# Lag convolution as three half-length ones; patch transforms with 64 rows of weights for each dim

## The reference, cut to what matters

```
x = x + conv_of_rational_filter(gn(x))      # layer 0: full linear 2-D convolution, 16 x 16 channels
x = x + patch_layer(gn(x))                  # layer 1: 8x8 patches, queries, keys, values
x = x + conv3x3(gn(x))                      # layer 2
x = x + conv_of_rational_filter(gn(x))      # layer 3: as layer 0, other filters
```

```
X = rfft2(x, s=(256, 256)); Y = einsum('...hwi,ijhw->...hwj', X, h0 + rfft2(h)[0]); y = irfft2(Y)[:128, :128]
```

## Time and profile before

| | us |
|---|---|
| median of 3 runs | 4166.98 |
| profiled execution | 4160.19 |
| its span, first to last instruction | 4158.3 |
| granted TensorE clock, share of full speed | 0.952 |

### The profile page before, as it was taken

How to read it: one execution, slowest core, us unless ns; L and a number is a source line. 1 busy time by engine, 2 the same in 40 slices (tenths; PEclk the granted TensorE clock), 3 DMA queues, 4 the chain that set the end, 5 groups by cost and what they waited for, 6 DMA issues and landing times. The chain is left out here.

```text
span 4158.3 us, 76077 instructions
## 1 busy us (share of the span) xinstructions
PE 3687.6 (89%) x32456; PEld 2790.0 (67%) x32456; DVE 1537.0 (37%) x1765; ACT 1506.1 (36%) x1559; POOL 994.6 (24%) x1002
## 2 busy tenths in 40 slices
PE   8999999759999769999888979999889977798997
PEld 8888888726555557777577767777567764465655
DVE  7665656231111033333444453333454454211111
ACT  2665656521111024444343445445344431211110
POOL 6665656200000013333243003333234000000000
PEclk9999999979999879999999999999999998999998
DMA  2344444476554352212122432112121443855455
GB/s 68 115 133 128 135 128 136 133 211 182 141 163 140 98 149 80 81 40 81 41 81 66 131 109 81 60 61 81 41 63 65 111 128 42 214 154 162 140 143 131
DMA packets 223117, 462.62 MB, mean 111 GB/s; under 512 B 30042, under 2 KB 109156, under 8 KB 205036
## 3 DMA queue, kind: packets, MB, share of 16 engines
q1 hardware_dynamic: 211036, 437.18, 36.5%
q10 hardware_dynamic: 11792, 21.12, 1.6%
HBM read 341.32 MB, written 113.77 MB: 109 GB/s over the span
## 5 line engine op out<-in xcount | busy, mean ns | idle before, releaser
L648 PE MATMUL c_acc<-c_shifted,c_filt 128*32 128x512 f32 (+7 forms) x16384 | 957.4, 396 | 99.2 <-issue 62.8
L648 PEld LDWEIGHTS c_acc<-c_shifted,c_filt 128*32 128x32 f32 x16384 | 602.0, 137 | 456.1 <-issue 307.7
L700 ACT ACTIVATE c_filt<-c_filt 64x2048 f32<-64x2048 f32 (+1 forms) x64 | 121.9, 1905 | 826.2 <-DMA c_filt<-filters_dram 826.2
L240 PE MATMUL f_ab<-f_taps_ab,f_table 65*128 (+1 forms) x2080 | 296.4, 303 | 19.2 <-DMA f_table<-const_taps 8.2
L240 PEld LDWEIGHTS f_ab<-f_taps_ab,f_table 65*128 65x128 f32 x2080 | 277.8, 215 | 32.2 <-issue 22.7
L342 ACT ACTIVATE f_stage<-f_far 128x512 f32<-128x512 f32 x256 | 256.9, 1078 | 16.8 <-PE f_far L132 8.7
L664 DVE COPY c_filt<-c_filt 64x2048 f32<-64x2048 f32 (+1 forms) x64 | 77.6, 1213 | 480.2 <-DMA c_filt<-filters_dram 480.2
L125 POOL TENSOR_TENSOR q_w_q<-raw_weights,q_w_q 128x2048 fp32r<-128x2048 f32 x2 | 11.5, 5752 | 967.4 <-ACT q_w_q L121 967.4
L130 PE MATMUL q_acc_q<-xn,q_w_q 128*128 128x512 f32 x512 | 201.0, 393 | 40.0 <-DVE xn L125 40.0
L1104 POOL TENSOR_TENSOR sums<-sums,store 128x512 f32<-128x512 f32 x64 | 176.8, 2763 | 233.3 <-DVE store L1048 233.3
L405 DVE RECIPROCAL f_rec<-f_mag 128x256 f32<-128x256 f32 (+1 forms) x144 | 228.7, 1588 | 2.2 <-POOL f_mag L432 2.2
(11 more groups left out here) (181 smaller groups left out, 7772.3 us busy)
## 6 DMA issues: line engine op xcount, KB each, us to landing
c_shifted<-spectrum_dram SPq DMA_DIRECT2D x64, 1054.0 KB, 10.7
filters_dram<-f_stage SPq DMA_DIRECT2D x128, 512.0 KB, 4.1
c_filt<-filters_dram SPq DMA_DIRECT2D x64, 1024.0 KB, 8.2
raw_weights<-in_L_conv_Wk SPq DMA_DIRECT2D x16, 2048.0 KB, 8.2
raw_weights<-in_L_conv_Wv SPq DMA_DIRECT2D x16, 2048.0 KB, 8.2
o_raw<-in_L_conv_Wout SPq DMA_DIRECT2D x128, 256.0 KB, 3.7
f_table<-const_taps SPq DMA_DIRECT2D x120, 260.0 KB
raw_weights<-in_L_conv_Wq SPq DMA_DIRECT2D x15, 2048.0 KB, 8.2
```

The lines of the kernel that those rows point to most:

```text
L240: mm = nc.tensor.matmul(ab[blk % 2][:, k, part], table[:, blk % 2, k, part], taps_ab[:, q], start=True, stop=True)
L648: mm = nc.tensor.matmul(acc[k][32 * s:32 * s + 32, :, lag:L], filt[:, k, h, :, :, KB * s + kb].rearrange("p j c -> p (j c)"), shifted[:, k ...
```

## The change

```diff
 LAGS = 4
-ROW = L + LAGS
+HALF = L // 2
+ROW = 2 * (HALF + LAGS)
...
     ang = tau * np.outer(n, n) / L
-    inv_h = np.stack([np.cos(ang), np.sin(ang), -np.sin(ang)], 1)[:, :, ::-1] / L
+    lag_order = [8 * (15 - k) + 2 * (3 - l) + phase for k in range(16) for phase in range(2) for l in range(4)]
+    inv_h = np.stack([np.cos(ang), np.sin(ang), -np.sin(ang)], 1)[:, :, lag_order] / L
...
                 act.wait_ge(freq_ready, u + 1)
                 if u >= 4:
                     act.wait_ge(stored[u % 4], 32 * (u // 4))
-                nc.scalar.activation(rows[:, u % 4, :, LAGS:ROW], freq[u % 2][:], ACT.Copy).then_inc(rows_ready, 1)
+                nc.scalar.activation(rows[:, u % 4, :, :, LAGS:], freq[u % 2][:].rearrange("p b (t q) -> p b q t", q=2), ACT.Copy).then_inc(rows_ready, 1)
...
-def convolve(nc, layer, scratch, tag):
-
-
-    KB, RING, HALVES = L // 8, 4, 2
+def convolve(nc, layer, spare, scratch, tag):
+
+
+    KB, RING = HALF // LAGS, 4
+    N_BATCHES = GROUPS // RING
     RUN = 4 * B * ROW - LAGS
+    EVEN, ODD, SUM = range(3)
     with ExitStack() as ctx:
         sb, ps, sem = allocators(nc, ctx, tag)
-        filt = sb("filt", [128, RING, HALVES, C, 2, 4 * KB])
-        shifted = sb("shifted", [128, RING, 4, B, ROW])
-        out = sb("out", [128, RING, B, L])
-        acc = [ps(f"acc{k}", [128, B, L]) for k in range(RING)]
+        filt = sb("filt", [128, RING, 3, C, 2, 4 * KB])
+        shifted = sb("shifted", [128, RING, 4, B, 2, HALF + LAGS])
+        total = spare[:, 0].rearrange("p r n -> p (r n)").rearrange("p (k m t) -> p k m t", k=RING, t=HALF)
+        out = spare[:, 1].rearrange("p r n -> p (r n)")[:, 0:RING * B * L].rearrange("p (k b t q) -> p k b t q", k=RING, b=B, q=2)
+        odd = sb("odd", [128, 2, B, 1 + HALF])
+        both = sb("both", [128, 2, B, HALF])
+        acc = [[ps(f"acc{k}{phase}", [128, 2 * B, HALF]) for phase in range(3)] for k in range(2)]
         filt_in = [sem(f"filt_in{k}") for k in range(RING)]
         rows_in = [sem(f"rows_in{k}") for k in range(RING)]
-        group_done, acc_out = sem("group_done"), [sem(f"acc_out{k}") for k in range(RING)]
-        negated, copied, cleared = sem("negated"), sem("copied"), sem("cleared")
+        filt_summed, rows_summed, negated, copied, cleared = (sem(n) for n in (
+            "filt_summed", "rows_summed", "negated", "copied", "cleared"))
+        halves_done, group_done, odd_out, both_ready, acc_out = (sem(n) for n in (
+            "halves_done", "group_done", "odd_out", "both_ready", "acc_out"))
...
         def load(eng, g, k):
-            eng.dma_start(filt[0:64, k].rearrange("p h j c n -> p h (j c n)"),
-                          scratch["filters"][bass.ds(g, 1), :, 4 * layer:4 * layer + 4].rearrange("o (h p) q j n -> p (o h) (q j n)", h=HALVES)
+            eng.dma_start(filt[0:64, k, EVEN:SUM].rearrange("p h j c n -> p h (j c n)"),
...
-        def block_of(k, lower, column, first):
-
-            return filt[64 * lower:64 * lower + 64, k, :, :, column, KB * first:4 * KB].rearrange("p h j n -> p (h j) n")
+        def ahead(n, k):
+
+            return (n, 3) if k == 0 else (n + 1, k - 1)
+
+        def filters_of(k, phases, lower, column, first):
+
+            return filt[64 * lower:64 * lower + 64, k, phases, :, column, KB * first:4 * KB].rearrange("p h j n -> p (h j) n")
...
         @block.tensor
         def _(pe):
-            def groups(n):
+            def product(k, phase):
+                for kb in range(KB):
+                    for s in range(4):
+                        rows = total[:, k, B * s:B * s + B] if phase == SUM else shifted[:, k, s, :, phase]
+                        mm = nc.tensor.matmul(
+                            acc[k % 2][phase][32 * s:32 * s + 32, 0:B, LAGS * kb:HALF],
+                            filt[:, k, phase, :, :, KB * s + kb].rearrange("p j c -> p (j c)"),
+                            rows[:, :, 0:HALF - LAGS * kb], start=kb == 0, stop=kb == KB - 1)
+                return mm
+
+            def group(n, k):
+                pe.wait_ge(rows_in[k], 16 * (n + 1))
+                pe.wait_ge(negated, 2 * (RING * n + k) + 1)
+                pe.wait_ge(copied, 2 * (RING * n + k) + 1)
+                if isinstance(n, int) and n == 0:
+                    if k == 0:
+                        pe.wait_ge(cleared, 2)
+                    if k >= 2:
+                        pe.wait_ge(acc_out, k - 1)
+                else:
+                    pe.wait_ge(acc_out, RING * n + k - 1)
+                product(k, EVEN)
+                product(k, ODD).then_inc(halves_done, 1)
+                pe.wait_ge(negated, 2 * (RING * n + k) + 2)
+                pe.wait_ge(copied, 2 * (RING * n + k) + 2)
+                pe.wait_ge(rows_summed, RING * n + k + 1)
+                product(k, SUM).then_inc(group_done, 1)
+
+            for k in range(RING):
+                group(0, k)
+            with pe.Fori(1, N_BATCHES) as n:
...
-                    pe.wait_ge(rows_in[k], 16 * (n + 1))
-                    pe.wait_ge(negated, RING * n + k + 1)
-                    pe.wait_ge(copied, RING * n + k + 1)
-                    if isinstance(n, int):
-                        if k == 0:
-                            pe.wait_ge(cleared, 2)
-                    else:
-                        pe.wait_ge(acc_out[k], n)
-                    for kb in range(KB):
-                        for h in (1, 0):
-                            lag = 8 * kb + LAGS * (HALVES - 1 - h)
-                            for s in range(4):
-                                mm = nc.tensor.matmul(
-                                    acc[k][32 * s:32 * s + 32, :, lag:L],
-                                    filt[:, k, h, :, :, KB * s + kb].rearrange("p j c -> p (j c)"),
-                                    shifted[:, k, s, :, 0:L - lag], start=lag == 0, stop=lag == L - LAGS)
-                    mm.then_inc(group_done, 1)
-
-            groups(0)
-            with pe.Fori(1, GROUPS // RING) as n:
-                groups(n)
+                    group(n, k)
...
+        @block.gpsimd
+        def _(pool):
+            def sums(n, k):
+                pool.wait_ge(filt_in[k], 16 * (n + 1))
+                nc.gpsimd.tensor_tensor(filt[0:64, k, SUM], filt[0:64, k, EVEN], filt[0:64, k, ODD], ALU.add).then_inc(filt_summed, 1)
+                pool.wait_ge(rows_in[k], 16 * (n + 1))
+                rows = shifted[:, k].rearrange("p s b q t -> p (s b) q t")
+                nc.gpsimd.tensor_tensor(total[:, k], rows[:, :, 0, 0:HALF], rows[:, :, 1, 0:HALF], ALU.add).then_inc(rows_summed, 1)
+
+            for k in range(RING):
+                sums(0, k)
+            with pool.Fori(1, N_BATCHES) as n:
+                for k in range(RING):
+                    sums(n, k)
...
         @block.vector
         def _(dve):
             def copy(n, k):
 
+                first = isinstance(n, int) and n == 0 and k == 0
                 dve.wait_ge(filt_in[k], 16 * (n + 1))
-                first = isinstance(n, int) and n == 0 and k == 0
-                nc.vector.tensor_copy(block_of(k, 1, 1, first), block_of(k, 0, 0, first)).then_inc(copied, 1)
+                nc.vector.tensor_copy(filters_of(k, slice(EVEN, SUM), 1, 1, first), filters_of(k, slice(EVEN, SUM), 0, 0, first)).then_inc(copied, 1)
+                dve.wait_ge(filt_summed, RING * n + k + 1)
+                nc.vector.tensor_copy(filters_of(k, slice(SUM, 3), 1, 1, first), filters_of(k, slice(SUM, 3), 0, 0, first)).then_inc(copied, 1)
 
             def drain(n, k):
+                dve.wait_ge(odd_out, RING * n + k + 1)
+                nc.vector.tensor_tensor(both[:, k % 2], acc_of(k, EVEN), odd[:, k % 2, :, 1:], ALU.add).then_inc(both_ready, 1)
+                dve.wait_ge(stored[k], 16 * (n + 1))
+                nc.vector.tensor_tensor(out[:, k, :, :, 0], acc_of(k, EVEN), odd[:, k % 2, :, 0:HALF], ALU.add)
+
+            def finish(n, k):
                 dve.wait_ge(group_done, RING * n + k + 1)
-                if not isinstance(n, int):
-                    dve.wait_ge(stored[k], 16 * n)
-                nc.vector.tensor_copy(out[:, k], acc[k][:]).then_inc(acc_out[k], 1)
+                dve.wait_ge(both_ready, RING * n + k + 1)
+                nc.vector.tensor_tensor(out[:, k, :, :, 1], acc_of(k, SUM), both[:, k % 2], ALU.subtract).then_inc(acc_out, 1)
...
             def dc_and_nyquist():
 
                 dve.wait_ge(filt_in[0], 16)
+                dve.wait_ge(filt_summed, 1)
                 nc.vector.tensor_copy(filt[64:128, 0, :, :, 1, 0:KB], filt[0:64, 0, :, :, 1, 0:KB]).then_inc(cleared, 1)
                 nc.vector.memset(filt[64:128, 0, :, :, 0, 0:KB], 0.0)
                 dve.wait_ge(cleared, 1)
                 nc.vector.memset(filt[0:64, 0, :, :, 1, 0:KB], 0.0).then_inc(cleared, 1)
 
+            nc.vector.memset(odd[:, :, :, 0:1], 0.0)
             dc_and_nyquist()
+            for k in range(3):
+                copy(0, k)
```

(47 more changed lines are left out.)

34 lines of the change are left out of this document (14 added, 20 removed).

## The result

The changed kernel takes 4199.5 us (median; 4198.3 to 4202.7, 4 runs) against 4165.4 us (4161.8 to 4175.8) for the kernel before, run beside it: ratio 1.0079 [1.006, 1.0098]. It is slower, by 0.8%; 3944 was forecast.

A forecast was written before the change was run, and what follows sets the result against it. PE was taken as the bound (busy 89% of the span). 4160.2 - 181.8 + 13 - 0.6 + 2.4 - 55.7 = 3937.5 us as profiled, 3944 as median; range 3890 to 4045, the sum's own 3905 to 3985.

The forecast's parts named there:

- convolution, both layers: Lag convolution: three products of 3.86 us, 11.58 instead of 14.42 us for each of 64 groups, -181.8 us.
- start of the layers: PE's first convolution matmul waits for POOL's first sums and DVE's clearing and copies: +6.5 us, twice, +13 us.
- transforms: Correlation steps: paired 64-row matmuls run side by side, 1.74 us less in each of 32 steps, -55.7 us.
- rest: Finishing copy of each layer's last group shorter, -0.6 us; spectrum stores 3% more, +2.4 us.
- above it whatever the pattern costs when it comes three times in a row: Lag convolution: open upper bound on the three products' time; its dearest reading was the rival at 4299 us.
- rival D: Lag convolution: PE runs out of instructions in small blocks; 5.0 us pause plus 2.4 slow clock per group, 4299; chance 0.03.
- the half with the small blocks ran through in 3.86 us: Evidence against instruction shortage: the old group's second half, 16 small blocks, in the earlier trace.
- 8.25 (10.1 with turns): POOL's two additions per convolution group: 8.25 us, plus 1.8 us taking turns with DVE's copies, under PE's 11.6.
- B: Lag convolution: POOL's additions late in part, period 14 to 16 us; at 15 us a group 4043; chance 0.12.
- C: Lag convolution: POOL bounds it at 16.6 us plus 1.8 in turns with DVE, 18.4 a group, 4262; chance 0.03.
- rival A: Transforms: row halves don't run side by side; 4031, or 4000 with no price for the split; chance 0.21.
- the price of the split: Transforms: changing the array's split costs 0.98 us per step; bounds 87 us gain without it, 31 us slower if unpaired.

The follow-up runs named there:

- e1: Changed kernel with the convolution loop's loads cut to a few numbers (64 of filters, 4 x 64 of rows; outputs wrong): 3965.5 us.
- e13: Kernel before the change, with its loop loads cut to a few numbers: 4156.6 us.
- e2: Changed kernel with POOL's two additions per group cut to a small part, all loads kept: 4186.7 us.
- e4: Kernel before with only the transforms' part of the change (64 rows of weights per dim): 4113.8 us, ratio 0.9878.
- e8: Changed kernel with each loop load cut into four by columns, same bytes in packets of about 2 KB: 4052.9 us.
- e3: Changed kernel with each loop load issued as four pieces by partitions, same bytes and 8 KB packets: 4307.4 us, ratio 1.033.
- e6: Changed kernel whose loop loads bring all rows but only 64 numbers of the filters: 4011.1 us.
- e12: Changed kernel with all filters loaded when the group ends and the rows only after the next group's second product: 4109.7 us.
- e14: Kernel before with PE's own loop over batches written out, loads unchanged: 4076.6 us, ratio 0.9788.
- e11: Changed kernel with loads spread over the group behind them in three issues, and PE's own loop written out: 3933.1 us, ratio 0.9434.

## Why the prediction was wrong, by its own steps

The forecast for the profiled execution was 3937.5; it took 4198.6, 261 us more. Measured against the kernel before, in us, from the windows and waits:

| term | forecast | measured |
|---|---|---|
| convolution, both layers | -181.8 | +62.8 |
| start of the layers | +13 | +25.9 |
| transforms | -55.7 | -47.2 |
| rest | +1.8 | -3.0 |

**The convolution is the step that failed**, in the sentence "above it whatever the pattern costs when it comes three times in a row", and in what rival D weighed against it: "the half with the small blocks ran through in 3.86 us". The miss is 244.6 us. In the two layers PE's idle time grew by 159.4 us (112.1 + 110.3 against 29.6 + 33.4), and its busy time fell by 96.6 instead of 181.8. Of these 85.2 us the 71 us that e1 has less come with the pauses: the matmuls behind them ran partly at 1.2 GHz. The rest, 14, is there in e1 as well; 12 of it is the product, 11.77 us a group instead of 11.58. The sum without the late fetch can be checked too: e1 is 28 us above 3937.5, some 10 for the convolution (both layers -171.7 instead of -181.8), 12 for the start of the layers and 8 for the transforms, less 2 for the rest.

Rival D had the right outcome (PE runs out of instructions) at 4299, with a chance of 0.03, and the wrong cause. It took the small blocks alone as the strain, and e1 shows that these run through (424.9 us for a layer, against 419 by the forecast's step). The strain is the small blocks beside a load, and the price is one pause a group, not three. The earlier trace rows had it in view: the window in which the small blocks "ran through", 1087.82 to 1091.68, has a DMA share of 0.00, and the large blocks before it 0.81. The one sample of the new pattern was taken without the traffic that three of them in a row must share the time with. I used that row as a rate and did not ask under what load it was measured. I also noted "PE runs out of instructions" without looking at how many arrive: 384 matmuls with their weight loads are 768 instructions per group in 11.6 us, three fetches, where the kernel before needed two in 14.4 us.

The Trainium skill, "Runtime: NRT & Kernel Launch", section "Instruction fetch mechanics", says that the store of instructions is refilled in blocks of 16 KiB by DMA and that this is mostly hidden. The blocks are as it says (301 packets, 4.93 MB); "mostly hidden" held in straight code of the kernel before (e13) and not in this one, where late fetches cost 163 us of PE's idle time over the run (221.8 us of "issue" against 58.5 in e1).

**The start of the layers** was forecast at +6.5 us each and came as +13: PE's idle time there is 31.4 instead of 18.55 us. POOL and DVE at the start of the first layer:

```profile
915.75 4.49 POOL L688 TENSOR_TENSOR c_filt<-c_filt 64x2048 f32<-64x2048 f32 x1 [159.09 <-DMA c_filt<-filters_dram]
920.20 2.34 POOL L691 TENSOR_TENSOR raw_weights<-c_shifted 128x1024 f32<-128x1024 f32 x1
...
920.35 2.61 DVE L724 COPY c_filt<-c_filt 64x768 f32<-64x768 f32 x1 [13.01 <-POOL c_filt L688]
...
923.83 4.50 POOL L688 TENSOR_TENSOR c_filt<-c_filt 64x2048 f32<-64x2048 f32 x1 [1.29 <-DMA c_filt<-filters_dram]
...
924.69 6.76 DVE L705 COPY c_filt<-c_filt 64x1536 f32<-64x1536 f32 x1
...
931.70 3.62 PE L654 MATMUL c_acc<-c_shifted,c_filt 128*32 128x256 f32 x36 [31.38 <-DVE c_filt L705]
```

The copies that I had at 0.5 and 0.95 us take 2.61 and 6.76: each ends just behind POOL's work. The exclusion seen in the earlier trace rows is there, but with the roles changed: POOL's additions keep their 4.5 and 2.3 us, and DVE's copy is held up. (Once at this start it went the other way: an addition that began at 931.83, beside a copy of 1.21 us, took 5.65 us.) In the groups it is as in the lines above (groups by shape, 985 to 1430; mean ns in the second number behind the bar):

```profile
L688 POOL TENSOR_TENSOR c_filt<-c_filt 64x2048 f32<-64x2048 f32 x26 | 118.0, 4538 | 275.1 <-DMA c_filt<-filters_dram 275.1
...
L705 DVE COPY c_filt<-c_filt 64x2048 f32<-64x2048 f32 x25 | 76.9, 3075 | 0.3
L691 POOL TENSOR_TENSOR raw_weights<-c_shifted 128x1024 f32<-128x1024 f32 x25 | 59.6, 2383 | 0.0
```

The copy has 3.1 us against 1.22; POOL's sum is 6.9 us against the 8.25 (10.1 with turns) that I took. So **rivals B and C** did not happen: PE's matmuls never wait for either in a group, and e2 is only 13 us faster, with its gain at the start of the layers. POOL's additions were priced by an fp32r one of 5.51 us; the plain fp32 one is 4.54.

**The transforms**: rival A falls. Row halves run side by side, and the price of the split was close: the gain was 47.2 us (53 by the runs of e4) of 55.7 forecast, between the bounds of 87 and -31.

**The side on which the range lay.** Chances of 0.94 for faster rested on the product at 3.86 us; C and D together had 0.05. D's price was a pause of 5.0 us and 2.4 of slow clock in each group; what came in most groups is one of 2.7 to 4.0 us and some 2 us lost to the slow clock, and none beside the last groups of a layer. A case of D weighed at what one undisturbed sample of 3.86 us is worth would have had far more than 0.03, and the range would have reached past 4165.

## What to carry to other kernels

Before a pattern is multiplied, look at the DMA share of the window that it was timed in, and count the instructions that PE then needs per us: here 256 instructions were used up in 3.9 us, and a fetch of the next 256 came 4.5 us late beside 2.1 MB queued in one go. If a kernel runs close to that, spread its loads over the work (three issues on PE's own milestones gave 217 us), or at least cut them into smaller packets (146 us here, e8); more pieces of the same packets, issued together, made it 108 us worse (e3). Idle PE time put down to "issue" inside straight code beside a busy DMA is the sign.

## What the hardware showed that I had not expected

- The fetch of PE's instructions that is wanted 3.7 us after the loads' issue (e1) begins 5.8 us after it beside the rows' 1.1 MB (e6), 7.3 us after it beside the filters' 1 MB (e12), and 8.2 us after it beside both (after). Of the delay, 1.2 us costs PE nothing.
- At each way back of its loop PE stood 4.3 to 5.4 us (before), with a slow clock behind it; writing the loop out gave 85 us on the kernel before (e14, 4161.4 to 4076.6) and 49 on the one with spread loads (e11).
- POOL's addition mostly keeps its time beside DVE's copy (25 of 25 in the middle of the first layer at 4.52 to 4.58 us), and the copy grows: from a forecast 0.95 to 6.76 us at the start of the layer, from 1.22 to 3.08 us in the groups.
